# Routed experts of the last batch: all experts on TensorE instead of scatter, load and add

## The chip, the cores and the metric

The kernel runs on one core of a Trainium2 chip. The metric is device time in microseconds of one execution. Five engines work beside each other: TensorE (PE), VectorE (DVE), ScalarE (ACT), GpSimd (POOL) and SyncE (SP), which here only issues DMAs. They meet through semaphores.

## What is computed

The input has 16 sequences of 375 rows and 128 channels. A token mixer, attention, a mixture of eight experts and a second attention come first and leave 345 tokens in each batch. The last layer, with which the change deals, routes each of the 5520 tokens to 8 of 64 experts. An expert takes the first 256 tokens that chose it, in token order; later ones are dropped.

```python
def _moe_forward(x, gate_w, gate_b, w1, w3, w2):          # CAP = 256, K = 8, E = 64
    x2 = x.reshape(-1, DIM)
    w, idx = _gate(x2, gate_w, gate_b)
    flat_e = idx.reshape(-1)
    oh = (flat_e[:, None] == jnp.arange(E)[None, :]).astype(jnp.int32)
    pos = (jnp.cumsum(oh, axis=0) * oh).sum(-1) - 1
    x_rep = jnp.repeat(x2, K, axis=0)
    xb = jnp.zeros((E, CAP, DIM), x2.dtype).at[flat_e, pos].set(x_rep, mode='drop')
    h = jax.nn.silu(jnp.einsum('ecd,edm->ecm', xb, w1)) * jnp.einsum('ecd,edm->ecm', xb, w3)
    yb = jnp.einsum('ecm,emd->ecd', h, w2)
    y = yb.at[flat_e, pos].get(mode='fill', fill_value=0.0) * w.reshape(-1)[:, None]
    return y.reshape(T, K, DIM).sum(1).reshape(shape)
...
h = h + _L1_ffn_ref(_layernorm(h, axis=-1), ...)
```

## The kernel before

The batches (`B` = 16, so 0 to 15) go through a software pipeline that is written out by hand: while one batch attends, the one before it is in its first mixture of experts, and the one before that is in the second attention and in the routing (`late`, 24 units on VectorE; the last units are the gate, the top 8, the counting against the capacity and the slot numbers). Tokens of a batch lie as 115 partitions by 3 (`A`, `J`).

The last layer works through DRAM. When a batch is routed, GpSimd stores its residual rows `h3` into `out` (`store_rows`) and scatters its rows (128 channels, 64 weights and the token's number) to `slots_dram`, 256 slots for each expert, with 24 indirect DMAs (`scatter`, `SENDS` = 24). Assignments beyond the capacity get a slot number out of bounds and are not written. Rows of even batches are counted on `rows_sent[0]`, those of odd ones on `rows_sent[1]`.

After the last batch come the experts. SyncE has loaded the weights of the first eight (`load_weights`), waits for both `rows_sent` (line 837) and loads the slots of experts 0 to 7 (`load_rows`, line 822); a later expert's rows and weights are loaded when the output of the one eight before it has been taken (`t_y`). For each expert TensorE turns the 256 rows (`expert_in`, line 1332), multiplies them with w1 and w3 (`expert_up`) and, after ScalarE's tanh (line 1584) and two steps on VectorE (`expert_h`, lines 2120 and 2121), with w2 (`expert_down`). `expert_y` on VectorE scales the output by the token's weight (line 2133) into one of eight buffers, once the add that last used it has landed. GpSimd adds it to the sum in DRAM with two indirect DMAs of 128 rows (`add_rows`, line 977): even experts to `out`, odd ones to `odd_sum_dram`, and an add waits for the one two experts before it. At the end one accumulating DMA joins the two sums (line 990). Experts 0 to 7 are written out; the other seven groups of eight are a loop, and each group runs to its end before TensorE starts the next. All of it is float32.

In the profile tiles have the names of the areas that they are cut from: expert rows and weights are `area_k`, outputs, tanh and copies `qv`, the hidden columns `area_h`; `W` stands for the PSUM banks W0 to W4, `Cb` for two more and `L` for the last.

## Time and profile before

| | us |
|---|---|
| median of 3 runs | 2299.24 |
| lowest and highest | 2298.69, 2302.49 |
| the profiled execution | 2305.26 |
| its span in the trace | 2303.4 |
| TensorE busy | 1959.6 (85%) |
| VectorE busy | 1457.8 (63%) |
| GpSimd busy | 741.2 (32%) |
| stretch from the last batch's routing to the end | about 310 |

The busy shares are means over the span. Up to about 1900 us the batches run and TensorE is busy nine tenths of the time; after that GpSimd is. In the rows "idle before" is the time in which an engine had nothing to do before an instruction, with what released it. A float32 product on TensorE appears as two records, and a record's length holds its passage through the array too, so that records overlap.

### The profile page before, as it was taken

To read this page: it belongs to the slowest core of one execution; us is meant where nothing else is said; L and a number is where in the kernel's file an instruction comes from. 1 tells how busy PE (TensorE), PEld (TensorE's weight loads), DVE (VectorE), ACT (ScalarE), POOL (GpSimd) and SP (SyncE) were. 2 spreads that over 40 slices of the span, in tenths; PEclk is the share of its full clock that TensorE was granted. 3 is DMA by queue.
4 is the path that set the end of the run, shared out by engine and by line. 5 is a ranking of instruction groups with operands and counts; after the bars stand their busy time and mean duration, and the time that the engine had idled before them with its cause. 6 is when DMAs were issued, how large, how long until landed. Compare 5 with 4: busy or idle time off the path is not lost. (4 is left out here: it accounts for less than half of the span.)

```text
span 2303.4 us, 46715 instructions
## 1 busy us (share of the span) xinstructions
PE 1959.6 (85%) x16960; PEld 1579.7 (69%) x16960; DVE 1457.8 (63%) x4386; ACT 863.2 (37%) x2193; POOL 741.2 (32%) x630
## 2 busy tenths in 40 slices
PE   3688999999999999999999999999988887266660
PEld 2677887888788788878887888788776565133440
DVE  4784465677677766776676766666666668344440
ACT  2453454444344434443434443434334341021120
POOL 1000000013132322323232323232325235768885
PEclk9999999999999999999999999999999899577775
DMA  6874744434344333423342424133200001057665
GB/s 213 277 265 135 252 160 146 144 121 130 93 125 126 111 105 109 124 86 115 94 129 68 121 83 127 50 117 93 80 2 10 6 4 25 8 108 126 115 92 72
DMA packets 167588, 251.52 MB, mean 109 GB/s; under 512 B 67379, under 2 KB 123011, under 8 KB 166608
## 3 DMA queue, kind: packets, MB, share of 16 engines
q10 hardware_dynamic: 43672, 153.59, 20.6%
q0 software_dynamic: 56688, 51.20, 10.4%
q1 hardware_dynamic: 67016, 43.91, 7.3%
q8 instruction: 133, 2.18, 0.4%
q14 instruction: 79, 0.65, 0.1%
HBM read 203.09 MB, written 87.40 MB: 126 GB/s over the span
## 5 line engine op out<-in xcount | busy, mean ns | idle before, releaser
L997 PE MATMUL Cb<-seq_hi,ring 128*128 128x174 f16 x4544 | 599.9, 240 | 20.9 <-DVE seq_lo L1669 10.7
L997 PE MATMUL Cb<-seq_lo,ring 128*128 128x174 f16 x2272 | 528.9, 240 | 0.0
L913 POOL DMA_INDIRECT slots_dram<-rows,slot_i x384 | 454.5, 1184 | 121.1 <-issue 121.1
L997 PEld LDWEIGHTS Cb<-seq_hi,ring 128*128 128x128 f16 x4544 | 405.2, 98 | 52.1 <-DVE seq_lo L1669 11.3
L1491 ACT ACTIVATE area_h<-W,nmax 115x345 f32<-115x345 f32 x384 | 210.3, 548 | 578.9 <-DVE nmax L1986 576.7
L997 PE MATMUL W<-area_k,qv 128*115 128x345 f32 (+1 forms) x1536 | 418.4, 462 | 4.1 <-ACT area_h L1491 2.4
L901 POOL TENSOR_TENSOR rstd<-ve,minus_half 115x3 f32<-115x3 f32 x64 | 59.1, 923 | 1103.4 <-DVE ve L1735 556.9
L1986 DVE TENSOR_REDUCE nmax<-W 115x1 f32<-115x345 f32 x384 | 196.7, 513 | 211.6 <-PE W L997 180.2
L997 PEld LDWEIGHTS Cb<-seq_lo,ring 128*128 128x128 f16 x2272 | 222.0, 98 | 16.5 <-issue 1.3
L1170 PEld LDWEIGHTS W<-ident,area_h 115*115 115x115 f32 x1152 | 165.5, 180 | 94.9 <-ACT area_h L1491 41.2
L1905 DVE SCALAR_TENSOR_TENSOR area_h<-area_h,W 128x345 f32<-128x345 f32 x256 | 131.6, 515 | 147.8 <-ACT area_h L1458 117.8
L997 PE MATMUL W<-w2eT,area_h 128*115 128x128 f32 x1536 | 193.9, 276 | 24.9 <-ACT area_h L1491 17.7
L997 PEld LDWEIGHTS W<-area_k,qv 128*115 128x115 f32 (+1 forms) x1536 | 159.1, 157 | 63.8 <-issue 11.9
L1170 PE MATMUL W<-ident,area_h 115*115 115x115 f32 x1152 | 182.9, 267 | 22.5 <-ACT area_h L1491 21.2
L997 PEld LDWEIGHTS W<-w2eT,area_h 128*115 128x115 f32 x1536 | 175.5, 179 | 35.6 <-issue 23.9
L997 PE MATMUL W<-mx_hl,w_hl 128*128 128x345 f16 x960 | 190.3, 313 | 5.2 <-DVE area_h L1905 3.7
L1497 ACT ACTIVATE area_k<-W 115x345 f32<-115x345 f32 x384 | 173.2, 451 | 12.0 <-PE W L1170 11.5
L1466 ACT ACTIVATE qv<-W,q_b 128x345 f32<-128x345 f32 x128 | 70.1, 549 | 231.9 <-PE W L997 231.7
L1458 ACT ACTIVATE area_h<-W 128x345 f32<-128x345 f32 x288 | 132.2, 459 | 21.4 <-DVE area_h L1905 13.6
L997 PE MATMUL W<-area_x,w_hl 128*128 128x345 f16 x576 | 118.7, 321 | 2.2 <-DVE area_k L1965 1.6
L997 PEld LDWEIGHTS W<-mx_hl,w_hl 128*128 128x128 f16 x960 | 93.9, 100 | 30.7 <-DVE area_h L1905 8.0
L1921 DVE SCALAR_TENSOR_TENSOR h<-W,comb,h 115x128 f32<-115x128 f32 x384 | 109.9, 342 | 1.6 <-PE L L997 0.5
(243 smaller groups left out, 2883.6 us busy)
## 6 DMA issues: line engine op xcount, KB each, us to landing
ring<-filters_dram ACTq DMA_DIRECT2D x252, 512.0 KB, 3.5
filters_dram<-ring ACTq DMA_DIRECT2D x36, 512.0 KB, 4.5
slots_dram<-in_empty_slots POOLq DMA_DIRECT2D x8, 1544.0 KB, 13.6
area_k<-slots_dram SPq DMA_DIRECT2D x64, 193.0 KB
band<-band_dram SPq DMA_DIRECT2D x64, 189.0 KB, 2.9
slots_dram<-rows,slot_i POOLq DMA_INDIRECT x384
x_win<-in_xpad SPq DMA_DIRECT2D x16, 252.0 KB
qv<-in_wc POOLq DMA_DIRECT2D x2, 1984.0 KB, 10.9
```

The lines of the kernel that those rows point to most:

```text
L901: pool.tensor_tensor(rstd[g][:, :], ve[g][:, :], minus_half[:, :], ALU.pow)\
L913: pool.indirect_dma_start(out=slots_d, out_offset=bass.IndirectOffsetOnAxis(ap=slot_i[parity(b)][:, m:m + 1], axis=0), in_=rows[parity(b)] ...
L997: return pe.matmul(o, l, r, start=start, stop=stop)
L1170: last = pe.transpose(w[0:A, i * A:(i + 1) * A], Pm[:, u % 2, i * A:(i + 1) * A], ident[0:A, 0:A])
L1458: act.activation(th[:, n % 2, :], bank[:, 0:TOK], ACT.Tanh, scale=0.5 / WS).then_inc(th_ready.h, 1)
L1466: act.activation(Q[:, h, :], bank[:, 0:TOK], ACT.Identity, bias=q_b[:, h:h + 1], scale=DH ** -0.5 / WS).then_inc(q_ready.h, 1)
L1491: act.activation(Pm[:, s % 2, :], bank[0:A, 0:TOK], ACT.Exp, bias=nmax[:, s % 2:s % 2 + 1], accum_out=psums[:, s // J, s % J:s % J + 1]).t ...
L1497: act.activation(pt_of(u), bank[0:A, 0:TOK].rearrange("p (i a) -> p i a", i=J), ACT.Copy)\
L1905: dve.scalar_tensor_tensor(dst, th[:, n % 2, :], 1.0, bank[:, 0:TOK], ALU.add, ALU.mult)\
L1921: ins = dve.scalar_tensor_tensor(dst[:, s], bank[0:A, s], scale, h1[:, s], ALU.mult, ALU.add)
L1986: dve.tensor_reduce(nmax[:, s % 2:s % 2 + 1], bank[0:A, 0:TOK], AX.X, ALU.max, negate=True).then_inc(nmax_ready.h, 1)
```

## The change

Batch 15 is not stored and scattered by GpSimd. SyncE waits for the scatters of batches 14 and 13 and loads the slots. The tokens of batch 15 stay in SBUF and meet all 64 experts: VectorE makes a table of their weights, zero where the token didn't choose the expert or came beyond the capacity (`d_chosen`), TensorE turns it, ScalarE copies it, SyncE stores it in DRAM, and loads two experts' rows of it at a time, each spread over 64 partitions (`load_wide`). Two experts have 2 x 64 hidden columns, so a pair is one product of 128x128 weights with 345 tokens for w1, one for w3 (`pair_up`) and one for w2 (`pair_down`), which adds to one PSUM bank over all 32 pairs. ScalarE has one step for a pair (`pair_tanh`), VectorE three (`pair_h`). At the end the sum is turned back and added to `h3`, and SyncE stores the rows into `out`; GpSimd waits for that store ahead of the join.

The experts of the other batches are one sequence of 64 without a loop: in each round of two, TensorE does up for experts g and g+1, down for g-4 and g-3 (`LAG_E`), and the pair before in between. To make room in PSUM, transposes have one bank instead of two, up two instead of four, outputs one instead of two. Adds, join, slots and buffers of outputs are as before.

```diff
+        e_w1 = [carve(0, 2 * F1).rearrange("p (r n) -> p r n", r=2) for _ in range(NE // 2)]
+        e_w3 = [carve(0, 2 * F1).rearrange("p (r n) -> p r n", r=2) for _ in range(NE // 2)]
         e_w2 = [carve(0, C)[0:F1, :] for _ in range(NE)]
+        e_w2p = [carve(0, C) for _ in range(NE // 2)]
...
+        e_wide = [carve(2, TOK) for _ in range(4)]
+        d_bank, d_acc = [W[1], L], Cb[1]
+        weights_d = nc.dram_tensor("weights_of_last_dram", (E1, TOK), F32, kind="Internal").ap()
...
-        up_bank = W[3:] + Cb
+        up_bank = W[3:]
+        turn_bank, y_bank = W[0], W[2]
...
+            def load_wide(n):
+
+                if n >= 4:
+                    sp.wait_ge(d_h_ready.h, d_h_ready.at(0, n - 4 + 1))
+                src = bass.AP(tensor=weights_d.tensor, offset=2 * n * TOK, ap=[[TOK, 2], [0, F1], [1, TOK]])
+                sp.dma_start(e_wide[n % 4], src).then_inc(d_wide[n % 4].h, 16)
+
+            def load_pair(n):
+                if n >= NE // 2:
+                    sp.wait_ge(d_added.h, d_added.at(0, n - NE // 2 + 1))
+                sp.dma_start(e_w2p[n % (NE // 2)], dram["w2e"][2 * n:2 * n + 2].rearrange("e f c -> (e f) c"))\
+                    .then_inc(d_load[n % (NE // 2)].h, 16)
...
-            for sig in rows_sent:
-                sp.wait_ge(sig.h, sig.at(B // 2 - 1, J * 8))
+            for n in range(NE // 2):
+                load_pair(n)
+
+            for sig, b in zip(rows_sent, (B - 2, B - 3)):
+                sp.wait_ge(sig.h, sig.at(pair_of(b), J * 8))
             for i in range(NE):
                 load_rows(0, i)
-            with sp.Fori(1, E1 // NE) as pr:
+            sp.wait_ge(d_wT.h, d_wT.at(0, 1))
+            sp.dma_start(weights_d, d_w).then_inc(s_weights, 16)
+            sp.wait_ge(s_weights, 16)
+            for n in range(4):
+                load_wide(n)
+            for pr in range(1, E1 // NE):
                 for i in range(NE):
+                    if i % 2 == 0:
+                        load_wide((pr * NE + i) // 2)
+                        load_pair((pr * NE + i) // 2)
                     sp.wait_ge(t_y.h, t_y.at(pr - 1, i + 1))
                     load_rows(pr, i)
                     load_weights(pr, i)
...
+            sp.wait_ge(d_out.h, d_out.at(0, 1))
+            sp.dma_start(bass.AP(tensor=out.tensor, offset=(B - 1) * TOK * C, ap=[[J * C, A], [1, J * C]]), h3[:, :])\
+                .then_inc(s_last, 16)
+            sp.wait_ge(s_last, 16)
...
-            store_rows(B - 1)
-            scatter(B - 1, 0, SENDS)
-            pool.wait_ge(h3_stored.h, h3_stored.at(B - 1, 1))
+            pool.wait_ge(h3_stored.h, h3_stored.at(B - 2, 1))
...
-            with pool.Fori(0, E1 // NE) as pr:
+            for pr in range(E1 // NE):
                 for i in range(NE):
                     add_rows(pr, i)
             for i in range(NE):
                 pool.wait_ge(t_out[i].h, t_out[i].at(E1 // NE - 1, 2))
+            pool.wait_ge(s_last, 16)
...
             def expert_in(pr, i):
...
+                if pr * NE + i >= 1:
+                    pe.wait_ge(t_xT.h, t_xT.at(pr, i))
                 for c in range(2):
-                    last = pe.transpose(turn_bank[i % 2][:, c * 128:(c + 1) * 128], e_rows[i][:, c, 0:C], ident[:, :])
+                    last = pe.transpose(turn_bank[:, c * 128:(c + 1) * 128], e_rows[i][:, c, 0:C], ident[:, :])
...
+                if pr * NE + i >= 2:
+
+                    pe.wait_ge(t_h.h, t_h.at(pr, i - 1))
+                mm(up_bank[i % 2][0:F1, 0:CAP], e_w1[i // 2][:, i % 2, :], e_xT[i % 2])
+                mm(up_bank[i % 2][0:F1, CAP:], e_w3[i // 2][:, i % 2, :], e_xT[i % 2]).then_inc(t_hps.h, 1)
...
+                if pr * NE + i >= 1:
+
+                    pe.wait_ge(t_y.h, t_y.at(pr, i))
...
-            def experts(pr, lag):
-                for i in range(0, NE + lag, 2):
-                    for k in i, i + 1:
-                        if k < NE:
-                            expert_in(pr, k)
-
-                    for k in i - lag, i - lag + 1:
-                        if k >= 0:
-                            expert_down(pr, k)
-                    for k in i, i + 1:
-                        if k < NE:
-                            expert_up(pr, k)
-
-            experts(0, 2)
-            with pe.Fori(1, E1 // NE) as pr:
-                experts(pr, 4)
+            def turn_weights():
+                pe.wait_ge(d_chosen.h, d_chosen.at(0, 1))
+                for j in range(J):
+                    last = pe.transpose(d_acc[0:E1, j * A:(j + 1) * A], sc[:, j, :], ident[0:A, 0:A])
+                last.then_inc(d_turned.h, 1)
+
+            def pair_up(n):
+
+                i = n % (NE // 2)
+                for k in 2 * i, 2 * i + 1:
+                    pe.wait_ge(t_load[k].h, t_load[k].at(2 * n // NE, 4))
+                if n >= 1:
+                    pe.wait_ge(d_h_ready.h, d_h_ready.at(0, n))
+                x = xTs[1][:, :]
+                mm(d_bank[0][:, 0:TOK], e_w1[i].rearrange("p r n -> p (r n)"), x).then_inc(d_full.h, 1)
+                mm(d_bank[1][:, 0:TOK], e_w3[i].rearrange("p r n -> p (r n)"), x).then_inc(d_full.h, 1)
+
+            def pair_down(n):
+                i = n % (NE // 2)
+                pe.wait_ge(d_load[i].h, d_load[i].at(0, n // (NE // 2) + 1))
+                pe.wait_ge(d_h_ready.h, d_h_ready.at(0, n + 1))
+                mm(d_acc[:, 0:TOK], e_w2p[i], d_h, start=(n == 0), stop=(n == E1 // 2 - 1)).then_inc(d_added.h, 1)
+
+
+            expert_in(0, 0)
+            turn_weights()
+            for g in range(0, E1 + LAG_E, 2):
+                if g >= LAG_E:
+                    expert_down((g - LAG_E) // NE, (g - LAG_E) % NE)
+                if g < E1:
+                    expert_up(g // NE, g % NE)
+                    expert_in((g + 1) // NE, (g + 1) % NE)
+                if g >= LAG_E:
+                    expert_down((g + 1 - LAG_E) // NE, (g + 1 - LAG_E) % NE)
+                if g < E1:
+                    expert_up((g + 1) // NE, (g + 1) % NE)
+                if 2 <= g <= E1:
+                    pair_down(g // 2 - 1)
+                if g + 2 < E1:
+                    expert_in((g + 2) // NE, (g + 2) % NE)
+                if g < E1:
+                    pair_up(g // 2)
+                if g == E1:
+                    pe.wait_ge(d_taken.h, d_taken.at(0, 1))
+                    for j in range(J):
+                        last = pe.transpose(d_bank[0][0:A, j * C:(j + 1) * C], d_sum[:, j * A:(j + 1) * A], ident[:, :])
+                    last.then_inc(d_back.h, 1)
...
+            def pair_tanh(n):
+                act.wait_ge(d_full.h, d_full.at(0, 2 * n + 1))
+                if n >= 1:
+                    act.wait_ge(d_h_ready.h, d_h_ready.at(0, n))
+                act.activation(d_th, d_bank[0][:, 0:TOK], ACT.Tanh, scale=0.5).then_inc(d_th_ready.h, 1)
+
+            expert_xT(0, 0)
+            act.wait_ge(d_turned.h, d_turned.at(0, 1))
+            act.activation(d_w, d_acc[0:E1, 0:TOK], ACT.Copy, scale=0.5).then_inc(d_wT.h, 1)
+            for g in range(0, E1 + 2, 2):
+                if g >= 2:
+                    pair_tanh(g // 2 - 1)
+                if g < E1:
+                    expert_tanh(g // NE, g % NE)
+                    expert_xT((g + 1) // NE, (g + 1) % NE)
+                    expert_tanh((g + 1) // NE, (g + 1) % NE)
+                if g + 2 < E1:
+                    expert_xT((g + 2) // NE, (g + 2) % NE)
+            act.wait_ge(d_added.h, d_added.at(0, E1 // 2))
+            act.activation(d_sum, d_acc[:, 0:TOK], ACT.Copy).then_inc(d_taken.h, 1)
...
+                elif unit == 23 and b == B - 1:
+
+                    dve.tensor_tensor(sc[:, :, :], rows[parity(b)][:, :, C:C + E1], mr[:, :, :], ALU.mult)\
+                        .then_inc(d_chosen.h, 1)
...
-            def experts(pr, lag):
-                expert.start(pr)
-                for i in range(0, NE + lag, 2):
-                    for k in i - lag, i - lag + 1:
-                        if k >= 0:
-                            expert_y(pr, k)
-                    for k in i, i + 1:
-                        if k < NE:
-                            expert_h(pr, k)
-
-            experts(0, 2)
-            with dve.Fori(1, E1 // NE) as pr:
-                experts(pr, 4)
+            pair = Chain(d_step)
+
+            def pair_h(n):
+                dve.wait_ge(d_th_ready.h, d_th_ready.at(0, n + 1))
+                pair.link(dve.scalar_tensor_tensor(d_s, d_th, 1.0, d_bank[0][:, 0:TOK], ALU.add, ALU.mult))
+                dve.wait_ge(d_full.h, d_full.at(0, 2 * n + 2))
+                pair.link(dve.tensor_tensor(d_s, d_bank[1][:, 0:TOK], d_s, ALU.mult))
+                if n >= 1:
+                    dve.wait_ge(d_added.h, d_added.at(0, n))
+                dve.wait_ge(d_wide[n % 4].h, d_wide[n % 4].at(0, n // 4 + 1))
+                dve.tensor_tensor(d_h, e_wide[n % 4], d_s, ALU.mult).then_inc(d_h_ready.h, 1)
+
+            for g in range(0, E1 + LAG_E, 2):
+                if g >= LAG_E:
+                    expert_y((g - LAG_E) // NE, (g - LAG_E) % NE)
+                if 2 <= g <= E1:
+                    pair_h(g // 2 - 1)
+                if g < E1:
+                    if g % NE == 0:
+                        expert.start(g // NE)
+                    expert_h(g // NE, g % NE)
+                if g >= LAG_E:
+                    expert_y((g + 1 - LAG_E) // NE, (g + 1 - LAG_E) % NE)
+                if g < E1:
+                    expert_h((g + 1) // NE, (g + 1) % NE)
+                if g == E1:
+                    dve.wait_ge(d_back.h, d_back.at(0, 1))
+                    dve.tensor_tensor(h3[:, :], h3[:, :], d_bank[0][0:A, 0:J * C], ALU.add).then_inc(d_out.h, 1)
```

TensorE, from the counting of batch 15 to the first experts; W0 and W1 hold transposes, W3, W4, Cb0 and Cb1 up, W2 and L outputs. Before:

```order
L997 MATMUL L<-sel,tri 115x64 x12
L1332 MATMUL W0<-ident,area_k 128x128 x2
L1332 MATMUL W1<-ident,area_k 128x128 x2
L997 MATMUL W3<-qv,area_k 64x256 x2
L997 MATMUL W4<-qv,area_k 64x256 x2
L1332 MATMUL W0<-ident,area_k 128x128 x2
L1332 MATMUL W1<-ident,area_k 128x128 x2
L997 MATMUL W2<-area_k,area_h 128x128 x2
```

Now the transposes of one expert stand ahead of its up, W1 and L are the pair's banks, and Cb1 takes the turned weights and the pair's sum:

```order
L1055 MATMUL L<-sel,tri 115x64 x12
L1390 MATMUL W0<-ident,area_k 128x128 x2
L1413 MATMUL Cb1<-ident,sc 64x115 x3
L1055 MATMUL W3<-qv,area_k 64x256 x2
L1390 MATMUL W0<-ident,area_k 128x128 x2
L1055 MATMUL W4<-qv,area_k 64x256 x2
L1390 MATMUL W0<-ident,area_k 128x128 x2
L1055 MATMUL W1<-xT1,area_k 128x345
L1055 MATMUL L<-xT1,area_k 128x345
L1055 MATMUL W3<-qv,area_k 64x256 x2
L1390 MATMUL W0<-ident,area_k 128x128 x2
L1055 MATMUL W4<-qv,area_k 64x256 x2
```

The first output (W2) moved from behind the up of two experts and the transposes of four to behind the up of four, the transposes of five and two pairs.

VectorE, from the last unit of the routing to the first output. Before:

```order
L1873 TENSOR_SCALAR slot_i1<-top 115x24
L2120 SCALAR_TENSOR_TENSOR qv<-qv,W3 64x256
L2121 TENSOR_TENSOR area_h<-W3,qv 64x256
L2120 SCALAR_TENSOR_TENSOR qv<-qv,W4 64x256
L2121 TENSOR_TENSOR area_h<-W4,qv 64x256
L2129 CAST qv<-area_k 128x2
L2133 TENSOR_SCALAR qv<-W2,area_k 128x128 x2
```

Now, from the same place, up to the hidden columns of the fourth expert and the first output:

```order
L1969 TENSOR_TENSOR sc<-rows1,mr 115x192
L2223 SCALAR_TENSOR_TENSOR qv<-qv,W3 64x256
L2224 TENSOR_TENSOR area_h<-W3,qv 64x256
L2223 SCALAR_TENSOR_TENSOR qv<-qv,W4 64x256
L2224 TENSOR_TENSOR area_h<-W4,qv 64x256
L2243 SCALAR_TENSOR_TENSOR area_h<-qv,W1 128x345
L2245 TENSOR_TENSOR area_h<-L,area_h 128x345
L2249 TENSOR_TENSOR area_h<-area_h 128x345
L2223 SCALAR_TENSOR_TENSOR qv<-qv,W3 64x256
L2224 TENSOR_TENSOR area_h<-W3,qv 64x256
L2223 SCALAR_TENSOR_TENSOR qv<-qv,W4 64x256
L2224 TENSOR_TENSOR area_h<-W4,qv 64x256
```

The first pair's three steps and two more experts' hidden columns moved in ahead of the first output; the third step (line 2249) reads two tiles that were cut from `area_h`.

GpSimd, from the end of batch 14's scatters. Before, with the store and the scatters of batch 15:

```order
L913 DMA slots_dram<-rows0,slot_i0 16384x193 x10
L907 DMA out<-h3 115x384
L913 DMA slots_dram<-rows1,slot_i1 16384x193 x24
L982 UNCONDITIONAL_BRANCH
L982 ISA
L974 ISA
L977 DMA out<-qv 5776x128 x2
```

Now the adds follow batch 14's scatters:

```order
L972 DMA slots_dram<-rows0,slot_i0 16384x193 x10
L1034 DMA out<-qv 5776x128 x2
L1034 DMA odd_sum_dram<-qv 5888x128 x2
```

Twenty-five DMAs left GpSimd's queue ahead of the adds.

## Rows read from the trace of the kernel before

**Rows 1.** The chain that ended last, 1850 to 2304 us, shares by line

```profile
by line: DMA odd_sum_dram<-qv 20.6%; issue 17.4%; DMA out<-qv 12.8%; POOL slots_dram L913 8.7%; PE W L997 8.4%; POOL odd_sum_dram L977 4.3%; PE L L997 1.4%; POOL out L977 1.2%; DVE area_h L1905 1.2%; DVE h L1921 0.9%; PE W L1332 0.9%; PE Cb
```

**Rows 2.** Timeline of GpSimd: start us, us, engine, line, operation [idle before]

```profile
1992.56 1.16 POOL L913 DMA_INDIRECT slots_dram<-rows,slot_i  x1 [0.30 <-issue]
...
1996.32 1.20 POOL L913 DMA_INDIRECT slots_dram<-rows,slot_i  x1 [2.00 <-issue]
...
2030.12 1.16 POOL L913 DMA_INDIRECT slots_dram<-rows,slot_i  x1 [0.30 <-issue]
2043.60 1.64 POOL L977 DMA_INDIRECT out<-qv  x1 [12.31 <-DVE qv L2133]
...
2279.72 1.55 POOL L977 DMA_INDIRECT odd_sum_dram<-qv  x1 [0.30 <-DMA out<-qv]
```

**Rows 3.** The adds' line 977 on GpSimd, 2040 to 2300 us: durations, who waited

```profile
L977 POOL DMA_INDIRECT odd_sum_dram<-qv x64: 1549/1553/1572, 2047.4 to 2279.7; - x64
...
  DVE qv L2129: 101.0, 44
...
DMA to landing us min/median/max: 3.2/3.3/4.3
```

**Rows 4.** The chain in order of time: start us, us, what

```profile
2030.12 2.36 DMA slots_dram<-rows,slot_i
2032.55 2.58 DMA area_k<-slots_dram
2035.18 1.25 PE W L1332 x4
```

**Rows 5.** Timeline of VectorE, the last step of the routing

```profile
1995.12 0.18 DVE L1873 TENSOR_SCALAR slot_i<-top 115x24 uint32<-115x24 f32 x1
```

**Rows 6.** Timeline of TensorE, first experts: start us, us of the whole group

```profile
2036.36 3.68 PE L997 MATMUL W<-qv,area_k 128*64 128x256 f32 x8
...
2041.02 0.75 PE L997 MATMUL W<-area_k,area_h 64*128 64x128 f32 x4
...
2061.42 1.94 PE L997 MATMUL W<-qv,area_k 128*64 128x256 f32 x8
2063.29 0.66 PE L1332 MATMUL W<-ident,area_k 128*128 128x128 f32 x4
```

**Rows 7.** Float32 products of 345 columns: two records (timeline), and the page's mean

```profile
1641.38 0.77 PE L997 MATMUL W<-area_k,qv 128*115 128x345 f32 x2
...
L997 PE MATMUL W<-area_k,qv 128*115 128x345 f32 (+1 forms) x1536 | 418.4, 462 | 4.1 <-ACT area_h L1491 2.4
```

**Rows 8.** Groups by line and shape, 1930 to 2304: busy us, mean ns of one

```profile
L1580 ACT ACTIVATE qv<-W 128x256 f32<-128x256 f32 x64 | 22.2, 382 | 129.8 <-PE W L1332 129.5
L2133 DVE TENSOR_SCALAR qv<-W,area_k 128x128 f32<-128x128 f32 x64 | 19.5, 349 | 0.0
L2120 DVE SCALAR_TENSOR_TENSOR qv<-qv,W 64x256 f32<-64x256 f32 x32 | 13.2, 411 | 48.8 <-ACT qv L1584 46.6
L1458 ACT ACTIVATE area_h<-W 128x345 f32<-128x345 f32 x14 | 6.4, 460 | 17.4 <-DVE area_h L1905 12.6 <-PE W L997 4.7
```

**Rows 9.** Timeline of SyncE's queue: the w1 load of two experts in a row

```profile
2045.63 0.33 SPq L826 DMA_DIRECT2D area_k<-in_w1e  x1
...
2047.84 0.33 SPq L826 DMA_DIRECT2D area_k<-in_w1e  x1
```

**Rows 10.** Stretches: PE, PEld, DVE, ACT, POOL busy us; granted clock, DMA share, GB/s

```profile
2034.00:2038.00 4.00, 2.82 (x8) 1.55 (x9) 0.00 (x0) 0.77 (x2) 0.00 (x0) 0.50 0.91 259
...
2046.00:2050.00 4.00, 3.79 (x23) 2.45 (x21) 3.08 (x11) 1.40 (x4) 3.40 (x3) 1.00 0.95 172
...
2094.00:2098.00 4.00, 1.19 (x4) 0.93 (x4) 1.47 (x6) 0.00 (x0) 3.39 (x3) 0.50 0.67 114
```

**Rows 11.** Timeline: VectorE's product of two SBUF operands and the scatter beside it

```profile
1919.72 0.52 DVE L1751 TENSOR_TENSOR mx_hl<-xT,mx_hl 128x345 f16<-128x345 f32 x1
...
1919.82 1.46 POOL L913 DMA_INDIRECT slots_dram<-rows,slot_i  x1 [0.30 <-issue]
```

54 lines of the change are left out of this document (28 added, 26 removed).

## The prediction

> **What bounds the kernel now.** I read the chain of waits for the last quarter first. It runs through GpSimd: the scatters of routed rows, then the expert adds and their DMAs [rows 1]. The timeline of GpSimd gives this part its dates [rows 2]. The last scatter for batch 14 starts at 1992.56 us. The 24 scatters of batch 15 stand one behind the other, the first at 1996.32 and the last at 2030.12. Then the engine idles until the first expert's output is ready, and the first add starts at 2043.60. From there 128 adds (two for each of 64 experts) follow without a hole: the last starts at 2279.72, so they are 236.12 / 127 = 1.859 us apart, 1.55 us of it the instruction [rows 3]. VectorE waited for adds to land 44 times, 101.0 us together [rows 3]: the experts' work runs ahead of the adds and is held back by them. So the stretch is set by when the first add starts, plus 128 add slots, plus 2303.4 - 2279.72 = 23.7 us for the last landing and the join of the two sums.
>
> The two steps between a last scatter and the first matmul of the experts are in the chain: 2.36 us until the rows landed, 2.58 us for their load, with TensorE starting at 2035.18, that is 5.06 us after the last scatter began [rows 4].
>
> **Part 1: the scatter of batch 15 goes.** SyncE then waits for batch 14's scatters. The last of these starts at 1992.56, so by the same distance TensorE can start its first expert at 1992.56 + 5.06 = 1997.6 instead of 2035.2, 37.6 us earlier. What is late next is the routing of batch 15 on VectorE, whose last step started at 1995.12 [rows 5]; the changed kernel has one 115x192 product there instead of it, so its weights are ready around 1995, before TensorE wants them. Nothing on TensorE stands in between: its next instruction after the counting is the experts' first.
>
> **Part 2: a longer fill before the first add.** Before, the first add came 2043.60 - 2035.18 = 8.4 us after TensorE's start. Now the output of expert 0 comes in the third round of two experts, behind much more work. The clock stands at half speed for some 6 us after the idle time: eight half-matmuls of 64x256 took 3.68 us at 2036.36 and 1.94 us later, and an output product at 2041.02 already took 0.75 us for its four halves, near what it takes later too; two experts' transposes take 0.66 us at full speed [rows 6]. Two half-matmuls of 345 columns in float32 take 0.77 us with 0.46 us for one alone, so they follow at 0.31 us, and one product of the new kind is 0.62 us of TensorE at full speed and about 1.2 at half [rows 7]. Half speed: expert 0's transposes 0.6, three transposes of the weights 0.9, expert 0's up products 1.85, expert 1's transposes 0.6, a wait of some 0.8 for ScalarE to copy them, up products 1.85: 6.6 us. Then at full speed: transposes 0.4 and first pair's up 1.3 (8.3); second round 1.0 + 0.3 + a wait of 0.9 for ScalarE, which now has the pair's tanh first, + 1.0 + 0.6 + 0.3 + 1.3 (13.7); expert 0's output product 0.7 (14.4). VectorE adds 0.9 (14.4 + 0.9 = 15.3), and 1.0 us lies between its end and the add, as between the end of VectorE's routing at 1995.30 and the first scatter at 1996.32 [rows 2, 5]. The first add starts 16.3 us after TensorE, at 2013.9. If the clock stays at half speed all through, the same list gives about 22 us (2019.6).
>
> The pair's weights also have a path: product on VectorE, transposes, copy, a store to DRAM by SyncE, a wait, a load spread over 128 partitions. Two transfers of some 2.5 us (the rows' load is the nearest row [rows 4]) behind eight row loads of 0.2 MB each, 6 us at the 259 GB/s of that moment [rows 10]: some 9 us after TensorE's start. VectorE needs them at about 10 us, so I cost this at nothing; without that cover it is up to 3 us.
>
> **Part 3: the steady rounds.** For two experts GpSimd gives 4 x 1.859 = 7.43 us. TensorE at full speed needs 0.66 for transposes, 1.94 for up, 1.5 for down [rows 6], and new 3 x 0.62 for the pair: 6.0 us. At half speed it is about 11 us. ScalarE: two copies, two tanh at 0.38 and one at 0.46, 2.0 us. VectorE: four steps at 0.41, two outputs of 0.9 (two products of 0.35 and a small cast), three steps of 345 columns at 0.52: 5.0 us [rows 8, 11]. SyncE: 2.21 us of issue for one expert [rows 9], plus two new issues, bounded by 0.4 and 0.6 us each, about 5.5 us. All are under 7.43. Fewer PSUM banks (one for transposes, one for outputs, two for up) put waits between the engines. I went through a round: the second output product waits for VectorE to take the first (0.9 us), and 1.3 us of other matmuls lie between them; the pair's third step on VectorE is done about 3.3 us into the round, and its product stands at 3.7. So the waits cost about 0.3 us and a round stays near 6.2. Experts are ready up to eight ahead, so a late one has some 20 us of cover. The unrolled loops remove register work only, which nothing waited for. Cost: nothing.
>
> DMA: per two experts the new loads bring 0.24 MB to about 0.58 MB. The 16 engines were 0.95 busy at 2046 to 2050 us, and GpSimd still worked 3.40 of 4 us [rows 10]. An add waits for the one two experts back on its table; it lands 3.3 us (3.2 to 4.3) after its last issue [rows 3], and 5.6 us are free for that. Cost: nothing.
>
> **Part 4: VectorE and GpSimd at one memory.** The third step of a pair multiplies two operands that both lie in SBUF, 128x345; in the stretch of the adds nothing of this kind ran before. The nearest row is a 128x345 product of two SBUF operands at 1919.72: the scatter that began 0.1 us after it took 1.46 us, others 1.16 [rows 2, 11]. So a collision at the start of a GpSimd instruction costs 0.30 us. With 32 such steps of 0.52 us and starts 1.86 us apart a quarter would collide: 32 x 0.28 x 0.30 = 2.7 us. Bounds: 0 if the phases miss, 32 x 0.30 = 9.6 us if each hits. The Trainium skill, SBUF — State Buffer, section Who interferes with whom, says that a VectorE instruction with two SBUF inputs contends with a GpSimd instruction that reads SBUF, and that the later one is blocked until the first ends. By that rule a step could cost its whole 0.52 us, 16.6 us for all 32, if it met every one; the row shows 0.30 of it, and only where the step came first.
>
> **Part 5: the end.** Batch 15's sum is turned back and stored in the round after expert 63's start. VectorE gets there when the add of expert 52 has landed, with 11 experts' adds, about 41 us, still to go; the store is one transfer. Hidden. The join stays.
>
> **Sum**, in the profiled execution: first add from 2043.60 to 2013.9 is -29.7 us; contention +2.7; together -27.0. Its span goes from 2303.4 to 2276.4, its time from 2305.3 to 2278.3. The median of the runs is 2299.24, 6 us under the profiled one; taken from it: **2272.2 us**.
>
> **Rivals.** (a) *The rounds don't keep up, a little*: a wait between engines that I have missed makes a round 7.43 to 8.2 us. For it: banks cut from two and four to one and two. Against: 1.2 us of slack after all that I found. At 8.0 us the 32 rounds cost 18 us: 2290. (b) *TensorE stays at half speed, slower than before*: a round is then 11 us against 7.43. In the old stretch the clock did fall: 0.50 at 2094 to 2098, where TensorE was busy 1.19 of 4 us, waiting for VectorE and through it for adds; it was 1.00 where it was busy 3.8 to 4.0 [rows 10]. One round at half speed takes 3.5 us off the lead; the change turns into a loss when more than (27 + 20) / 3.5 = 13 of 32 rounds are at half speed, and all 32 would give 2272 + 113 - 20 = 2365. Against it: the new work keeps TensorE busy 6.0 of 7.43 us evenly, where the old one came in bursts of eight experts, and at half speed it would never be idle, which is when the rows show full speed coming back. (c) *Every pair's third step hits an add*, since VectorE is woken by landings and so may keep in phase with GpSimd: 9.6 instead of 2.7 us, 2279. (d) *The saving does not arrive*: the spread weights come late and hold VectorE and through it expert 0, or the clock stays low in the fill: first add at 2020, 2278.
>
> **Chances.** Forecast with its near misses (2266 to 2276) 0.60; (c) and (d), alone or together, 2276 to 2285, 0.25; (a) 0.10; (b) 0.05. The range 2266 to 2285 leaves out (a), (b) and little else. A change under 0.2% (4.6 us) can't be told from none; faster by more than that 0.93, within it 0.02, slower 0.05.
>
> **What would show it.** Right: no scatter after 1993.7; first add at 2012 to 2016; adds 1.86 to 1.88 us apart to the end; VectorE still waiting for adds; granted clock near 1.00 in the stretch; the last store long before the join. Wrong: holes between adds with TensorE or VectorE as releaser (a), a clock of 0.5 with TensorE never idle (b), add instructions of 1.8 us (c), the first add past 2018 (d).

## The result: slower by 0.7%

| | before | after |
|---|---|---|
| median, us | 2299.44 | 2317.86 |
| lowest to highest | 2298.69 to 2302.49 | 2316.90 to 2322.37 |
| span of the profiled execution | 2303.4 | 2315.8 |

The ratio of the times is 1.0073, with a 95% interval of 1.0061 to 1.0085. The forecast was 2272.2 us and its range ended at 2285: the time moved the other way, and the forecast is off by 45.7 us.

GpSimd's timeline in the trace of the changed kernel gives the dates that [rows 2] gave before (start us, us, engine, line, operation, idle before):

```profile
1987.35 1.16 POOL L972 DMA_INDIRECT slots_dram<-rows,slot_i  x1 [0.30 <-issue]
2010.15 1.63 POOL L1034 DMA_INDIRECT out<-qv  x1 [21.64 <-issue]
2012.08 1.57 POOL L1034 DMA_INDIRECT out<-qv  x1 [0.30 <-issue]
2013.96 1.55 POOL L1034 DMA_INDIRECT odd_sum_dram<-qv  x1 [0.31 <-issue]
2015.81 1.55 POOL L1034 DMA_INDIRECT odd_sum_dram<-qv  x1 [0.30 <-DMA out<-qv]
2019.24 1.55 POOL L1034 DMA_INDIRECT out<-qv  x1 [1.89 <-issue]
2021.10 1.55 POOL L1034 DMA_INDIRECT out<-qv  x1 [0.30 <-issue]
2022.95 1.55 POOL L1034 DMA_INDIRECT odd_sum_dram<-qv  x1 [0.31 <-issue]
2024.81 1.55 POOL L1034 DMA_INDIRECT odd_sum_dram<-qv  x1 [0.30 <-issue]
2028.25 1.78 POOL L1034 DMA_INDIRECT out<-qv  x1 [1.89 <-DMA out<-qv]
```

The first add starts at 2010.15, 33.45 us earlier than before. But the adds now have holes. An expert's add begins at 2010.15, 2019.24 and 2028.25 for the same table, so a round of two experts takes 9.0 us where it took 7.43. The row of the adds' line (min/median/max of the instruction in ns, first and last start; below it the time to landing) stands against [rows 3]:

```profile
L1034 POOL DMA_INDIRECT odd_sum_dram<-qv x64: 1546/1547/1811, 2014.0 to 2292.4; - x64
...
DMA to landing us min/median/max: 3.2/5.3/7.6
```

The instruction is as short as before, but what it sends off lands after 5.3 us at the median and 7.6 at most, where it was 3.3 and 4.3. (These figures rest on 48 of the 128 adds here and on 16 before, and they mix the records of an expert's two adds.) The trace also keeps up to 16 landing records for each add, 32 for an expert, a few of them missing. Read one by one, an expert's last landing came at the median 5.9 us after its second add began (at most 7.6), and 3.7 us before the change (at most 4.5). Up to 2150 us, among the 24 experts with all 32 records, the 28th of them came after 3.8 us and the last after 6.2; before it was 3.4 and 3.6. So it is the last four of 32 that are late, which fits two for each add.

From the first add to the last it is 2292.42 - 2010.15 = 282.3 us, against 236.1: +46.2. With the first add at -33.45 that makes +12.7, and the span grew by 12.4. So everything that is to be explained lies in the distance of the adds. (The median grew by 6 us more than the span, because the profiled execution of before was 6 us above its median.)

Later in the stretch a hole is larger. GpSimd at 2160, then VectorE at the same place, where `expert_y` wants a buffer back from an add:

```profile
2162.91 1.55 POOL L1034 DMA_INDIRECT out<-qv  x1 [0.30 <-issue]
2167.49 1.55 POOL L1034 DMA_INDIRECT odd_sum_dram<-qv  x1 [3.03 <-issue]
2169.34 1.55 POOL L1034 DMA_INDIRECT odd_sum_dram<-qv  x1 [0.30 <-issue]
...
2242.39 1.55 POOL L1034 DMA_INDIRECT out<-qv  x1 [0.30 <-DMA odd_sum_dram<-qv]
2244.24 1.55 POOL L1034 DMA_INDIRECT out<-qv  x1 [0.30 <-issue]
2246.09 1.55 POOL L1034 DMA_INDIRECT odd_sum_dram<-qv  x1 [0.31 <-issue]
```

```profile
2156.60 0.17 DVE L2232 CAST qv<-area_k 128x2 uint32<-128x2 f32 x1 [3.58 <-DMA odd_sum_dram<-qv]
...
2166.73 0.17 DVE L2232 CAST qv<-area_k 128x2 uint32<-128x2 f32 x1 [5.19 <-DMA odd_sum_dram<-qv]
```

VectorE is woken by a landing at 2166.73, and GpSimd starts the next add of that table at 2167.49, 0.76 us later; the last landing record lies at 2166.65, 0.83 or 0.84 us ahead of GpSimd's start. That GpSimd's hole says "issue" and not "DMA" must not mislead: the landing had come, and the time from there to the start is put down to no one. From 2240 on the holes are gone (SyncE's last load of spread weights is at 2230.2, below, its last load for an expert at 2240.2), and the adds are again 1.85 us apart.

SyncE's queue at the start, and then the row of the new loads' line:

```profile
1989.73 3.97 SPq L851 DMA_DIRECT2D area_k<-slots_dram  x8
1994.09 0.47 SPq L886 DMA_DIRECT2D weights_of_last_dram<-area_h  x1
1997.85 11.12 SPq L864 DMA_DIRECT2D area_h<-weights_of_last_dram  x5
```

```profile
L864 SPq DMA_DIRECT2D area_h<-weights_of_last_dram x32: 493/535/4512, 1997.9 to 2230.2; - x32
```

Between 2004.5 and 2007.5 only such loads are under way. The view of the DMAs in that stretch (GB/s; share of the 16 engines; what was issued):

```profile
DMA packets 107, 0.16 MB, mean 54 GB/s; under 512 B 0, under 2 KB 106, under 8 KB 106
...
q1 hardware_dynamic: 106, 0.15, 13.2%
...
area_h<-weights_of_last_dram SPq DMA_DIRECT2D x2, 172.5 KB
```

13.2% of 16 engines is 2.1 engines. A load of 128 rows ran on about two engines, at 54 GB/s, though others were issued behind it; eight row loads in the trace of before had run at 259 [rows 10]. The landing records say the same: a later load of this kind leaves two of them, 6.6 to 9.7 us after its issue, and one more about 1 us after it, where an add leaves 16. At that rate one load of 172.5 KB holds its two engines for 3.3 us (worked out). I took this as the suspect.

### The profile page after: what moved, and what is told of

It reads as the page before. It is cut to its first block and busy times, and to the rows that moved or that the text cites. A ratio compares the mean times of both kernels' runs of the same rounds, so it can differ in the third digit from the quotient of the medians.

```text
span 2315.8 us, 46676 instructions
## 1 busy us (share of the span) xinstructions
PE 2027.9 (88%) x17158; PEld 1605.0 (69%) x17158; DVE 1497.8 (65%) x4479; ACT 881.2 (38%) x2227; POOL 712.8 (31%) x605
## 5 line engine op out<-in xcount | busy, mean ns | idle before, releaser
L972 POOL DMA_INDIRECT slots_dram<-rows,slot_i x360 | 426.9, 1186 | 112.0 <-issue 108.3
L1055 PEld LDWEIGHTS Cb<-seq_lo,ring 128*128 128x128 f16 x2272 | 221.4, 97 | 16.4 <-issue 1.3
L1547 ACT ACTIVATE area_h<-W 128x345 f32<-128x345 f32 x288 | 132.2, 459 | 21.4 <-DVE area_h L2008 13.6
L1034 POOL DMA_INDIRECT odd_sum_dram<-qv x64 | 99.3, 1552 | 56.9 <-issue 53.2
## 6 DMA issues: line engine op xcount, KB each, us to landing
area_h<-weights_of_last_dram SPq DMA_DIRECT2D x32, 172.5 KB
```

Of the source, the lines that this page charges most:

```text
L972: pool.indirect_dma_start(out=slots_d, out_offset=bass.IndirectOffsetOnAxis(ap=slot_i[parity(b)][:, m:m + 1], axis=0), in_=rows[parity(b)] ...
L1034: pool.indirect_dma_start(out=sums[i % 2], out_offset=bass.IndirectOffsetOnAxis(ap=e_idx[i][:, c:c + 1], axis=0), in_=e_y[i][:, c, :], in_ ...
L1055: return pe.matmul(o, l, r, start=start, stop=stop)
L1547: act.activation(th[:, n % 2, :], bank[:, 0:TOK], ACT.Tanh, scale=0.5 / WS).then_inc(th_ready.h, 1)
```

## Experiments

The first four ran on one chip (before: 2300.57 us). The other eight ran on a second Trainium2 chip, on which every kernel is slower in the batches: before took 2365.02 us (2350.35 to 2377.49, 13 runs) beside the second four and 2368.02 (2366.24 to 2373.61) beside the last four. So only ratios, stretches and differences within a set are compared. The times in us that the expectations of the second set name are those of the first chip, so they are read as ratios to 2299.4 us. "Stretch" is first to last start of an add.

### First set: which part costs it

**e1_no_wide**: spread weights only for the first four pairs.

```diff
-                        load_wide((pr * NE + i) // 2)
...
-                dve.wait_ge(d_wide[n % 4].h, d_wide[n % 4].at(0, n // 4 + 1))
+                if n < 4:
+                    dve.wait_ge(d_wide[n % 4].h, d_wide[n % 4].at(0, 1))
```

> The changed kernel, but the spread weights are loaded for the first four pairs only and used again for the others, so the sum of batch 15 is left wrong; all other work is the same. In the changed kernel an add lands 5.5 to 5.9 us after its last issue (3.3 before) and two experts' adds take 9.0 to 10 us instead of 7.43. Theory W (the spread loads, 172.5 KB for two experts, hold up the adds' DMAs): landing goes back to 3.5 to 4.5 us, rounds to 7.4 to 7.8 us, time 2265 to 2280. Theory B (any added bytes do it, by amount): 73% of the added bytes go, most of the loss goes, 2275 to 2290. Theory S (the even sequence of row loads beside adds does it, not the added loads): landing stays at 5.5 and the time above 2305.

**e2_no_pair_w2**: the same with `load_pair` (line 894) and its wait (line 1429).

> The changed kernel, but the second copy of w2 for a pair (64 KB) is loaded for the first four pairs only, so the sum of batch 15 is left wrong. Theory W: nearly no change, 2310 to 2320, landing 5.5 us. Theory B: a quarter of the loss of 45 us goes, about 2306. Theory S: no change, 2315 to 2320. If SyncE's queue is what bounds the rounds (its issue of this load takes 1.8 us in the median, up to 3.8), the rounds get 1 to 2 us shorter, 2270 to 2290.

**e3_neither**: both. 

> The changed kernel with both of the added loads for the first four pairs only; all products of the pairs are still made (sum of batch 15 wrong). Theories W and B: the full gain of the prediction, 2262 to 2277, adds 1.86 us apart, landing 3.3 to 4. Theory S: above 2300, rounds still 9 us. If TensorE or VectorE set the rounds: no better than 2310 and holes between adds released by VectorE.

**e4_before_without_last**: the kernel before without the scatter of batch 15, and without anything in its place.

```diff
-            for sig in rows_sent:
-                sp.wait_ge(sig.h, sig.at(B // 2 - 1, J * 8))
+            for sig, b in zip(rows_sent, (B - 2, B - 3)):
+                sp.wait_ge(sig.h, sig.at(pair_of(b), J * 8))
...
-            scatter(B - 1, 0, SENDS)
```

> The kernel before, but batch 15 is stored and not scattered, and SyncE waits for the scatters of batches 14 and 13; batch 15's experts are left out, nothing is added. It measures part 1 of the prediction alone: first add 37 us earlier than before, time 2262 (2299.4 - 37); adds still 1.86 us apart, landing 3.3 us. A rival: without the scatter of batch 15 something else is late, then 2270 to 2290.

| | us | ratio to before, 95% | first add | stretch | landing min/med/max |
|---|---|---|---|---|---|
| changed kernel | 2317.86 | 1.0073 [1.0061, 1.0085] | 2010.15 | 282.3 | 3.2/5.3/7.6 |
| e1 | 2279.80 | 0.9909 [0.9877, 0.9941] | 2015.88 | 241.5 | 3.2/3.7/5.8 |
| e2 | 2322.18 | 1.0093 [1.0064, 1.0123] | 2012.05 | 284.1 | 3.2/5.1/6.5 |
| e3 | 2278.66 | 0.9904 [0.9875, 0.9933] | 2013.14 | 240.3 | 3.2/3.6/6.2 |
| e4 | 2265.29 | 0.9846 [0.9817, 0.9875] | 2004.00 | 236.3 | 3.2/3.4/4.9 |

The adds' row with its landings in the traces of e1 and of e2:

```profile
L1033 POOL DMA_INDIRECT odd_sum_dram<-qv x64: 1548/1548/1811, 2019.7 to 2257.3; - x64
...
DMA to landing us min/median/max: 3.2/3.7/5.8
```

```profile
L1033 POOL DMA_INDIRECT odd_sum_dram<-qv x64: 1547/1548/1807, 2015.9 to 2296.1; - x64
...
DMA to landing us min/median/max: 3.2/5.1/6.5
```

The 28 later loads of spread weights cost nearly all of it: without them the stretch is 40.8 of the 46.2 us shorter, and without both kinds only 1.2 us shorter still. Leaving out the pairs' w2 loads gave nothing back (e2), neither the quarter of the loss that theory B asked for nor what a full queue on SyncE would have given. In e1 and e3 all the new work on TensorE, VectorE and ScalarE is there with its fewer banks, and their stretch is 5.3 and 4.1 us over that of before. So the new work and its waits are nearly hidden, and theory S falls by e1, B by e2. e4 says what the scatter of batch 15 was worth by itself: 35.3 us of the time, for 37 expected. (In its profile the first add came 39.6 us earlier, 2.0 of it because batch 14's last scatter already was that much earlier.)

These runs take away bytes too, 4.9 MB of them in e1. That it is the form of the load and not its size they don't show.

### Second set: the load's form, and the load alone

**e5_two_loads**: the same bytes in two loads of 64 rows.

```diff
-                src = bass.AP(tensor=weights_d.tensor, offset=2 * n * TOK, ap=[[TOK, 2], [0, F1], [1, TOK]])
-                sp.dma_start(e_wide[n % 4], src).then_inc(d_wide[n % 4].h, 16)
+                for r in range(2):
+                    src = bass.AP(tensor=weights_d.tensor, offset=(2 * n + r) * TOK, ap=[[0, F1], [1, TOK]])
+                    sp.dma_start(e_wide[n % 4][r * F1:(r + 1) * F1, :], src).then_inc(d_wide[n % 4].h, 16)
```

> The changed kernel with one thing other: each load of spread weights (128 rows, the first 64 all reading one row of the table in DRAM, the last 64 the next row) is issued as two loads of 64 rows with one outer dimension of 64, where it was one load with an outer dimension of 2. The same bytes into the same places, one instruction more on SyncE. Theory N (narrow load): with an outer dimension of 2 a load runs on two DMA engines and blocks them for some 3.7 us, and the adds, which are spread over all 16, land late (median 5.3 us, up to 7.6). Over 16 engines the same bytes go by quickly: adds land at 3.3 to 4.2 us at the median, a round of two experts' adds takes 7.4 to 7.9 us, the stretch of adds 236 to 250 us, the whole 2268 to 2285 us. Rival H (reading one row of DRAM 64 times over is what is slow, or the bytes as such, 172.5 KB a load): landing stays at 5 us or more, the stretch at 275 us or more, the whole at 2305 us or more. Between the two if both take part.

**e7_before_more_narrow** and **e8_before_more_broad**: the kernel before with the same load added for each pair of experts, read by nobody. It reads two rows of `w1e` 64 times each, and SyncE waits for the load four pairs back before it issues the next. In e7:

```diff
+                src = bass.AP(tensor=dram["w1e"].tensor, offset=2 * n * TOK, ap=[[TOK, 2], [0, F1], [1, TOK]])
+                sp.dma_start(e_more[n], src).then_inc(more[n].h, 16)
```

and in e8 the two lines in the form of e5.

> The kernel before with one load added for every two experts, which nobody reads: 128 rows of 345 numbers out of a table of weights in DRAM, in the form of the changed kernel's load (outer dimension 2), into buffers of its own. The scatter and all else are those of before, so that this measures the load alone. Theory N: the adds land at 4.7 to 6 us at the median where they landed at 3.3, a round of two experts' adds takes 8.5 to 9.5 us, the stretch of adds grows by 35 to 50 us, the whole is 2330 to 2350 us. Rival H: the same, since the bytes and the rows read are the same. Rival L (the load is innocent, and the changed kernel's adds are late by what TensorE and VectorE do for the last batch): 2299 to 2306 us.

> The kernel before with the same added bytes as its sister kernel, nobody reading them, but each load issued as two loads of 64 rows (outer dimension 64). Theory N: the adds land at 3.3 to 4.2 us at the median, the stretch of adds grows by at most 10 us, the whole is 2299 to 2310 us, and the two kernels lie 25 to 50 us apart. Rival H: no better than the sister kernel with the one load, 2330 to 2350 us.

**e9_two_loads_short_lag**: e5 with `LAG_E = 2`.

> The changed kernel with the loads of spread weights in two of 64 rows each, and the constant of the order of the experts LAG_E 2 instead of 4, so that an expert's product back and its add come two experts sooner behind its first product. Theory: the time from TensorE's start to the first add falls by the work on two experts and one pair that then lies behind it, 3 to 7 us of the 17.8 us, and the end moves with it if the adds, 3.7 us apart, remain what bounds the stretch: 2262 to 2280 us, 3 to 7 us under the kernel with the two loads and LAG_E 4. Rival Q: with two experts less in hand TensorE and VectorE, which already work some 6.2 us of a round of 7.4, give up their slack to one another, adds wait for them, a round grows by 0.2 us or more over 32 rounds, and nothing is gained or some us lost.

| | us | ratio to before, 95% | last scatter | first add | stretch |
|---|---|---|---|---|---|
| e5 | 2338.90 | 0.9893 [0.9840, 0.9946] | 2054.84 | 2076.14 | 238.1 |
| e7 | 2408.89 | 1.0186 [1.0116, 1.0255] | 2091.7 | 2104.8 | 277.3 |
| e8 | 2373.36 | 1.0040 [1.0010, 1.0070] | 2090.7 | 2103.8 | 237.5 |
| e9 | 2338.73 | 0.9885 [0.9833, 0.9937] | 2060.01 | 2076.35 | 238.5 |

GpSimd in e7 and then in e8 at the same time, in kernels that differ only in the form of a load that no instruction reads:

```profile
2213.09 1.55 POOL L988 DMA_INDIRECT out<-qv  x1 [1.54 <-DMA out<-qv]
2214.95 1.55 POOL L988 DMA_INDIRECT out<-qv  x1 [0.30 <-issue]
2217.11 1.55 POOL L988 DMA_INDIRECT odd_sum_dram<-qv  x1 [0.61 <-issue]
2218.97 1.55 POOL L988 DMA_INDIRECT odd_sum_dram<-qv  x1 [0.30 <-issue]
2222.03 1.55 POOL L988 DMA_INDIRECT out<-qv  x1 [1.51 <-DMA out<-qv]
```

```profile
2209.32 1.55 POOL L989 DMA_INDIRECT out<-qv  x1 [0.30 <-DMA odd_sum_dram<-qv]
2211.17 1.55 POOL L989 DMA_INDIRECT out<-qv  x1 [0.30 <-issue]
2213.03 1.55 POOL L989 DMA_INDIRECT odd_sum_dram<-qv  x1 [0.30 <-DMA out<-qv]
2214.89 1.55 POOL L989 DMA_INDIRECT odd_sum_dram<-qv  x1 [0.30 <-issue]
2216.75 1.55 POOL L989 DMA_INDIRECT out<-qv  x1 [0.31 <-issue]
```

A round is 2222.03 - 2213.09 = 8.94 us in e7 and 2216.75 - 2209.32 = 7.43 in e8. The same bytes over the same repeated rows make the stretch 39.8 us longer in one form than in the other (35.5 us in the times); over the 236.1 us of before, which is from the first chip, it is 41.2 us in e7 and 1.4 in e8. The landing records agree: an expert's last landing came at the median 6.0 us after its second add began in e7 and 3.7 in e8, and in e7 for the add pair at 2213.09 and 2214.95 the trace holds 27 records, of which 23 came by 3.1 us and the last two at 6.2. So theory N stands, and H falls. So does L, since e7 has none of the changed kernel's other work. The whole of e8 is 0.4% over before (8 us), which no hole between adds explains; the loads before the first add stand there too, and I leave it open.

In e5 the stretch is back at 238.1 us. The view of the DMAs from 2073 to 2076, in the repeat of e5 (e12, below), where again only these loads are issued:

```profile
DMA packets 368, 0.40 MB, mean 135 GB/s; under 512 B 75, under 2 KB 368, under 8 KB 368
...
q1 hardware_dynamic: 368, 0.40, 41.8%
...
area_h<-weights_of_last_dram SPq DMA_DIRECT2D x6, 86.2 KB
```

135 GB/s instead of 54, and 41.8% of the engines' time, more than two engines can give. (135 GB/s is no ceiling: SyncE issued one load of 86.2 KB about every 0.64 us there.) The Trainium skill, DMA: Bandwidth & Descriptors, section Why a DMA increments its semaphore by 16 and not by 1, has the rule: a DMA uses the largest number of engines up to 16 that divides the size of the slowest dimension, of both its sides, that isn't 1. The first form's slowest dimension is 2, so two engines by the rule; the trace agrees (13.2% of 16). The second's is 64, so 16, and there too the trace agrees: the first ten of these loads, of 64 rows, left 16 landing records each, where a load of 128 rows in the first form left two.

e5 also gives back the fill: the first add came 16.4 us after TensorE's start (2059.76), for 17.8 in the changed kernel, and VectorE no longer waited for the first spread weights. e9 missed what was expected of it, 3 to 7 us under e5: the times differ by 0.2 us. Its rounds did not grow (238.5 us for 238.1), so rival Q isn't the reason; the third set takes it up.

### Third set: what a late landing does, and all on one chip

**e10_after_again** is the changed kernel, **e12_two_loads_again** is e5, **e13_short_lag_again** is e9. **e11_four_tables** is the changed kernel with four tables for the adds and its narrow loads as they are:

```diff
-        sums = [out, odd_d]
+        more_d = [nc.dram_tensor(f"more_sum_dram{k}", (sum_rows, C), F32, kind="Internal").ap() for k in range(2)]
+        sums = [out, odd_d] + more_d
...
-                if i >= 2:
-                    pool.wait_ge(t_out[i - 2].h, t_out[i - 2].at(pr, 2))
+                if i >= 4:
+                    pool.wait_ge(t_out[i - 4].h, t_out[i - 4].at(pr, 2))
...
-                        out=sums[i % 2], out_offset=bass.IndirectOffsetOnAxis(ap=e_idx[i][:, c:c + 1], axis=0),
+                        out=sums[i % 4], out_offset=bass.IndirectOffsetOnAxis(ap=e_idx[i][:, c:c + 1], axis=0),
```

> The changed kernel once more, unaltered, so that it stands on one chip beside the kernel before and beside those with the loads in two. Both theories: 0.7 +- 0.3% slower than before on the same chip, as on the chip of the first measurement, and the adds some 9.0 to 10.1 us a round for two experts.

> The changed kernel with its narrow loads as they are, but four tables of sums in turn where it has two, so that an add waits for the landing of the one four experts back and no longer two; two of the tables are joined to nothing, so the sums of half the experts are missing in the output. It tells what a late landing costs by itself. Theory R (the late landing holds the next add of the same table back, and that alone makes the round longer): GpSimd issues at 1.85 us per instruction again, a round takes 7.4 to 7.8 us, the stretch of adds 236 to 250 us, the whole 0.985 to 0.993 of before, though the landings themselves stay late. Theory T (the two engines that carry the narrow load are full: 3.7 us for it and their share of everything else in each round, so that no round can be shorter than 9 us): the stretch stays at 270 us or more and the whole within 0.5% of the changed kernel, and the landings grow later still.

> The changed kernel with each load of spread weights issued as two of 64 rows, as in the run of that name, once more beside the changed kernel itself. Theory N: 0.986 to 0.993 of before, and 1.4 to 2.2% under the changed kernel on the same chip; stretch of adds 236 to 245 us. Rival H: no more than 0.5% under the changed kernel.

> The kernel with the loads in two and LAG_E 2, once more. In its profile the first add came 16.3 us behind the last scatter, 21.3 us with LAG_E 4, but its last scatter itself 5.2 us later, and the times were the same. Theory P (where the last scatter ends wanders by some us from one execution and one build to the next, and the 5 us of the fill are real): 3 to 7 us under the kernel with LAG_E 4 in this measurement. Theory V (the constant or the layout of the program moves the last scatter by those 5 us in every execution): equal to it within 2 us, and the last scatter again 5 us later in its profile.

| | us | ratio to before, 95% | last scatter | first add | stretch |
|---|---|---|---|---|---|
| e10, the changed kernel | 2387.98 | 1.0084 [1.0065, 1.0104] | 2053.6 | 2076.8 | 284.0 |
| e11 | 2347.16 | 0.9903 [0.9885, 0.9921] | 2058.3 | 2081.2 | 242.2 |
| e12 | 2344.67 | 0.9892 [0.9872, 0.9913] | 2059.3 | 2080.7 | 240.0 |
| e13 | 2336.41 | 0.9860 [0.9843, 0.9878] | 2057.4 | 2073.7 | 237.9 |

The adds of e11 in the middle of the stretch, narrow loads and all:

```profile
2153.62 1.55 POOL L1035 DMA_INDIRECT more_sum_dram<-qv  x1 [0.30 <-issue]
2155.47 1.55 POOL L1035 DMA_INDIRECT more_sum_dram<-qv  x1 [0.31 <-issue]
2157.33 1.55 POOL L1035 DMA_INDIRECT more_sum_dram<-qv  x1 [0.30 <-issue]
2159.18 1.55 POOL L1035 DMA_INDIRECT more_sum_dram<-qv  x1 [0.30 <-issue]
2161.03 1.55 POOL L1035 DMA_INDIRECT out<-qv  x1 [0.31 <-issue]
2162.89 1.55 POOL L1035 DMA_INDIRECT out<-qv  x1 [0.30 <-issue]
```

With an add free of the landing two experts back, there are no holes: 41.7 us of stretch come back, theory R. The two engines are not full, so T falls; what the narrow load takes from the others is time to landing. The landings stayed late all the same: by the landing records an expert's last one came 6.0 us after its second add began (median), as in the changed kernel. SyncE's queue is the same in e11, so it wasn't what held the rounds. Two of the four tables are not joined in e11, so what more tables would cost at the end is not in its time.

e12 lies 43.3 us (1.8%) under the changed kernel on the same chip, by the form of one load. e13 lies 8.3 us under e12: in its profile the first add came 16.3 us after the last scatter, as in e9, where e12 and e5 have 21.4 and 21.3. In the measurement of e9 and e5 the difference was 0.2 us. In the profiles the last scatter ended 5.2 us later in e9 than in e5, but 1.9 earlier in e13 than in e12, so that it wanders, and theory V falls. Theory P had 3 to 7 us, and neither 0.2 nor 8.3 lies in that; how much of the 8 us is the shorter lag's is uncertain, and the profiles' 5.0 us of fill are the better number.

## Why the prediction was wrong, step by step

**Part 1 (the scatter goes)** held. TensorE started at 1992.32, 4.97 us after the last scatter, for 5.06 in the sum. The last scatter of batch 14 itself was 5.2 us earlier in this execution than in that of before, which is luck and no part of the change: it moved by such amounts between kernels that are equal up to there, as the last scatters of e5 and e9 show. That is why the first add at 2010.15 lies even before the forecast 2013.9.

**Part 2 (the fill)** held: the first add came 17.8 us after TensorE, for 16.3. The 1.5 us are the first spread weights, for which VectorE waited in the row below: in e5 and e12, with the load in two, the wait is gone and the first add comes 16.4 us after TensorE. The sum had them some 9 us after TensorE's start; they came after 12.5, since the narrow loads themselves were slow. "Up to 3 us" was a sufficient bound, but not for that reason.

```profile
2004.83 0.52 DVE L2249 TENSOR_TENSOR area_h<-area_h 128x345 f32<-128x345 f32 x1 [2.74 <-DMA area_h<-weights_of_last_dram]
```

**Part 3, the engines' rounds**, held as far as e3 shows: with all this work and without the loads the stretch was 240.3 us, 4.1 over before, most of it from part 4 below. Rival (a) named longer rounds, but by waits between engines and up to 8.2 us.

**Part 3, the paragraph on DMA, is the step that failed**: "it lands 3.3 us (3.2 to 4.3) after its last issue, and 5.6 us are free for that. Cost: nothing." It cost nearly all of the 46.2 us by which the stretch grew in the profile: 41 to 44 us come back in e1, e12 and e5. There were three errors in it. I weighed the new loads by bytes and by the mean share of 16 engines, and never asked over how many engines one of them is spread; the diff shows `ap=[[TOK, 2], ...]`, and the Trainium skill's rule above, had I applied it, gives two. I took the landing from a trace without such loads, as if it were a constant. But an add leaves 16 landing records, the next add waits for the last of them, and beside a narrow load two of the 16 come late, in the changed kernel as in e7, where nobody reads the load. That these two are of the engines that carry the load is inferred from the count, since the records don't name the engine. And the free time was less than 5.6 us: from the last landing to the start of the next add pass 0.83 us at least, so it was 4.8. With an expert's last landing at 6.2 us (median up to 2150 us) a round is 6.2 + 0.83 + 1.85 = 8.9 us; 9.0 was measured.

**Part 4 (VectorE beside GpSimd)** was sized at 2.7 us. Where landings set the rounds it hardly shows: in the changed kernel two adds took some 1.8 us instead of 1.55. Where they don't, it is there at about the size forecast. In e3 twelve of the 128 adds were longer by 0.13 to 0.34 us, 3.0 us together (in e1 twelve, in e12 ten), and each of them began while the pair's third step was running; five more in e3 began in such a step and were not longer. From e3, GpSimd and then VectorE:

```profile
2054.00 1.82 POOL L1031 DMA_INDIRECT out<-qv  x1 [0.30 <-issue]
2056.13 1.55 POOL L1031 DMA_INDIRECT odd_sum_dram<-qv  x1 [0.30 <-DMA out<-qv]
```

```profile
2053.88 0.52 DVE L2248 TENSOR_TENSOR area_h<-area_h 128x345 f32<-128x345 f32 x1
```

Eight such adds in a row, some 5.8 us apart, begin 0.12 to 0.23 us behind the start of the step, so VectorE does keep in phase with GpSimd for a while, as rival (c) feared, but not for all pairs. One that began 0.13 us behind it, with 0.39 us of the step left, grew by 0.26 us, so it was held for less than the rest of the step. Adds that began just ahead of the step took 1.55 us in e3.

**Part 5** held: in e1, e3 and e5 the last add alone sets the end. **Rival (b)** didn't come true. In the rounds of 9.0 us the granted clock was 1.00 while the holes were there already, as the first row shows (stretch, then busy us and count of PE, PEld, DVE, ACT and POOL, granted clock, DMA share, GB/s); it was 0.76 between 2150 and 2200, where the rounds were 10.1 us. These too were set by landings and not by TensorE: the odd experts' last landing came 7.2 to 7.6 us after the second add's start there, and the next add of that table 0.83 us after it (in one of nine, 1.14), which makes 7.4 + 0.83 + 1.85 = 10.1.

```profile
2050.00:2100.00 50.00, 42.27 (x182) 23.20 (x182) 30.31 (x92) 13.83 (x35) 35.14 (x23) 1.00 0.74 147
...
2150.00:2200.00 50.00, 39.21 (x133) 22.14 (x134) 22.83 (x70) 9.74 (x25) 30.71 (x21) 0.76 0.73 109
```

With the load in two, the change brings nearly what was forecast for it: -1.1% in e5 and in e12 (interval of e12: -1.3 to -0.9), which is 23.4 us in e12, for 27.0 us or -1.2% in the sum. Open stays why the odd experts' landings went from some 6.2 to 7.4 us after 2147 in the changed kernel; that wasn't tried.

## What to carry to other kernels

Cost a transfer by how many DMA engines it runs on, not by its bytes: look at the outermost dimension of both its sides, and keep a small one (a broadcast over two rows) from standing outermost by cutting the transfer in pieces. A transfer on few engines costs those who share these engines, above all a chain in which the next step waits for a landing; so for a step that waits for landings write down how much later they may come, less the time from a landing to the next start, and look for what could use it up. Where such a chain can't be spared late landings, more buffers in turn (here four tables for two) hide them, at the price of joining them at the end, which no run here paid.

## What the runs showed of the hardware

- A load of 128 rows of 1380 bytes with an outer dimension of 2 ran at 54 GB/s on 13.2% of the 16 engines and left two late landing records; in two loads of 64 rows it was 135 GB/s and 41.8%, with 16 records for each load. SyncE was held at five of the former for 11.12 us.
- Beside such loads GpSimd's adds landed after 5.3 us at the median (7.6 at most) instead of 3.3, while the instructions stayed at 1.55 us. Of the 16 landing records of an add, two were late. A load that nobody read did this to the rounds as well (8.94 us against 7.43).
- From the last landing record of an add to the start of the GpSimd instruction that waited for it passed 0.83 to 0.85 us.
- An add that began while VectorE multiplied two SBUF operands of 128x345 took up to 0.34 us longer, mostly 0.26 (1.81 for 1.55 us; e1, e3, e12).
- Two Trainium2 chips differed by 2.8 to 3.0% for the same kernel. The changed kernel's last scatter started at 1987.35 us on one and at 2053.6 on the other, but the stretch of adds was 282.3 and 284.0 us, so that 66.3 of the 68.2 us by which the spans differ lie ahead of it, and the ratios to before agreed (1.0073 and 1.0084).
